# Other PSUM banks for the first two and the last groups of a four-stage transformer pipeline, with the order of both ends written anew

## The reference

```
x = x + cross_attention(ctx, ln(x), mask)        # 8 heads of 16, 77 keys, k and v are the halves of ctx
x = x + s2*(relu2(s1*relu2(s0*[z,-z]@K0)@K1)@K2) # z = ln(x); K0, K1, K2 are +1/-1 matrices, widths 512, 512, 128
x = x + depool(rmsnorm(ln(x))@W_in.T + b_in, rmsnorm(ctx)[..., :128], patch_lens)   # a decaying scan, picked by rank
x = x + top2_of_8_experts(ln(x))                 # softmax gate, 8 experts of 128x128, weighed sum of the best two
```

## Time and profile before

| | |
|---|---|
| median of 3 runs | 553.19 us (551.71 to 553.41) |
| the profiled execution's own time | 553.28 us |
| its span in the trace | 551.5 us |
| TensorE busy | 504.6 us, 92% of the span |
| VectorE busy | 429.6 us, 78% |
| GpSimd busy | 364.2 us, 66% |
| ScalarE busy | 355.7 us, 64% |
| mean granted TensorE clock | 0.982 of full speed |
| DMA | 31 GB/s on average, 16.98 MB |

### The profile page before, as it was taken

The page is one execution under the profiler, slowest core; times in us unless marked ns, Lnnn a source line. Parts: engine busy times, 40 slices in busy tenths (PEclk is TensorE's granted clock), DMA queues, the critical chain, the costliest instruction groups (busy, mean ns, idle before and its releaser), DMA issues.

```text
span 551.5 us, 15070 instructions
## 1 busy us (share of the span) xinstructions
PE 504.6 (92%) x5532; PEld 329.5 (60%) x5532; DVE 429.6 (78%) x1404; ACT 355.7 (64%) x761; POOL 364.2 (66%) x633
## 2 busy tenths in 40 slices
PE   2785898999999999999999999999999999889774
PEld 1565565766666576656676666657665657445531
DVE  7555659888897979797987979797879776865586
ACT  3889567877676867676777768686566565523310
POOL 7874035586868778686868686877758494744554
PEclk9999899999999999999999999999999999999888
DMA  7331001010110101010101001000000000000000
GB/s 167 95 76 43 1 20 50 2 49 21 29 42 20 49 4 49 21 49 22 50 20 49 23 26 44 21 26 3 26 2 8 20 1 22 1 20 1 21 19 19
DMA packets 28503, 16.98 MB, mean 31 GB/s; under 512 B 3687, under 2 KB 28429, under 8 KB 28430
## 3 DMA queue, kind: packets, MB, share of 16 engines
q1 hardware_dynamic: 26670, 15.57, 10.3%
q10 hardware_dynamic: 1760, 0.46, 0.4%
HBM read 11.74 MB, written 4.24 MB: 29 GB/s over the span
## 4 chain that ended last, share of the span: by engine, by line
PE 81%; DVE 7%; ACT 4%; issue 2%; POOL 0%; DVEq 0%; ACTq 0%; POOLq 0%
PE ps L1991 20%; PE ps L1939 20%; PE ps L1884 6%; PE ps L1950 5%; PE ps L1827 5%; PE ps L1901 5%; PE ps L1932 4%; PE ps L1969 3%; PE ps L1970 3%; PE ps L1909 2%; PE ps L1859 2%; DVE weighed L977 2%; PE ps L1982 2%; ACT xn L1480 2%; PE ps L1888 1%
## 5 line engine op out<-in xcount | busy, mean ns | idle before, releaser
L608 POOL TENSOR_TENSOR sum<-weighed 128x512 f32<-128x512 f32 x60 | 76.2, 1270 | 100.3 <-DVE weighed L977 100.3
L1991 PE MATMUL ps<-w_moeT,y4T 128*128 128x512 f32 x256 | 127.3, 624 | 1.5 <-DVE xd L923 0.8
L1939 PE MATMUL ps<-h,w 128*128 128x512 f16 x512 | 118.3, 380 | 2.2 <-DVE att L879 1.2
L977 DVE TENSOR_TENSOR weighed<-ps,wgt 128x1024 f32<-128x1024 f32 x64 | 77.8, 1219 | 42.2 <-PE ps L1991 41.3
L1569 ACT ACTIVATE h<-ps 128x512 f16<-128x512 f32 x128 | 73.7, 591 | 54.2 <-PE ps L1939 33.9
L900 DVE SCALAR_TENSOR_TENSOR h<-ps,h 128x512 f16<-128x512 f32 x128 | 84.7, 681 | 20.1 <-ACT h L1569 20.1
L1939 PEld LDWEIGHTS ps<-h,w 128*128 128x128 f16 x512 | 47.9, 98 | 57.3 <-issue 4.1
L1535 ACT ACTIVATE prT<-ps,maskT 77x1024 f32<-77x1024 f32 x64 | 67.4, 1102 | 16.6 <-PE ps L1888 16.6
L1991 PEld LDWEIGHTS ps<-w_moeT,y4T 128*128 128x128 f32 x256 | 46.7, 195 | 44.7 <-issue 36.9
L560 POOL TENSOR_TENSOR rs<-ve,neg_half 128x4 f32<-128x4 f32 x64 | 65.9, 1030 | 8.7
L848 DVE TENSOR_REDUCE mx<-ps 128x8 f32<-128x616 f32 x64 | 47.7, 786 | 6.3 <-PE ps L1859 6.1
(11 more groups left out here) (169 smaller groups left out, 981.8 us busy)
## 6 DMA issues: line engine op xcount, KB each, us to landing
cx<-in_ctx SPq DMA_DIRECT2D x16, 308.0 KB
xa<-in_x SPq DMA_DIRECT2D x16, 256.0 KB, 3.0
out_x<-xo SPq DMA_DIRECT2D x16, 256.0 KB, 2.3
plugs<-plug_d SPq DMA_DIRECT2D x16, 77.0 KB
nat<-in_L_ffn_W SPq DMA_DIRECT2D x1, 512.0 KB
k_u<-in_L_ffn_k ACTq DMA_DIRECT2D x1, 256.0 KB, 4.8
k_u<-in_L_ffn_k ACTq DMA_DIRECT2D x1, 128.0 KB, 2.5
k_u<-in_L_ffn_k ACTq DMA_DIRECT2D x1, 64.0 KB, 5.6
```

Of the source, the lines that this page charges most:

```text
L608: nc.gpsimd.tensor_tensor(sum4[:], both[:, 0:4 * D], both[:, 4 * D:8 * D], ALU.add).then_inc(c_sum4.sem, 1)
L977: nc.vector.tensor_tensor(weighed[:, j % 2, :].rearrange("p (e d) -> p e d", e=E), pm(g, j).rearrange("p b (e d) -> p (b e) d", d=D), wgt[ ...
L1939: last = pe.matmul(pb(g, k), w2[:, i, c * 128:(c + 1) * 128], h1[:, g.p, part, i, :], start=(i == 0 and part == 0), stop=(i == FC - 1 and ...
L1991: last = pe.matmul(pm(g, j)[:, half, :], y4T[:, g.p, j * S:(j + 1) * S], w_moeT[:, half * 512:(half + 1) * 512], start=True, stop=True)
```

## The change

Banks: g[0]'s attention moves from banks 0 to 3 to banks 4 to 7, and g[1]'s from 4 to 7 to 0 to 3. The turns of the last group move from bank 2 to 0 and its small products from 3 to 1; those of the group before it from 6 and 7 to 4 and 5. The experts of g[13] take two pairs of banks in turn, as g[14]'s did, and the last two pairs of g[15] change places. The lists of all engines are written anew at both ends, and in the middle a few calls change places with their neighbours. What each call does is not changed.

```
         def pa(g):
-            return ps[:, 4:8] if g.n == 1 else ps[:, 0:4]
+            return ps[:, 4:8] if g.n == 0 else ps[:, 0:4]
         def pb(g, k):
             return ps[:, (0 if g.n == NG - 1 else 4) + k % 2, :]
         def pt(g):
-            return ps[:, 2 if g.n == NG - 1 else 6, :]
+            return ps[:, {NG - 1: 0, NG - 2: 4}.get(g.n, 6), :]
         def pp(g):
-            return ps[:, 3 if g.n == NG - 1 else 7, :]
+            return ps[:, {NG - 1: 1, NG - 2: 5}.get(g.n, 7), :]
         def pm(g, j):
             b = 6
             if g.n == NG - 1:
-                b = (2, 6, 0, 4)[j]
-            elif g.n == NG - 2:
+                b = (2, 6, 4, 0)[j]
+            elif g.n >= NG - 3:
                 b = (6, 2)[j % 2]
             return ps[:, b:b + 2]
...
-            make_values()
-            make_ones()
-            a_values_in(g[0])
             rstd(ln_a, g[0])
             a_patch_scale(g[0])
+            rstd(ln_a, g[1])
+            make_values()
             a_patch_normalise(g[0])
-            rstd(ln_a, g[1])
+            a_values_in(g[0])
             make_signs()
             a_patch_scale(g[1])
             make_constants()
-            a_values_in(g[1])
-            a_patch_scale(g[2])
-            make_weights_to_turn()
+            make_ones()
...
+            b_low(g[14], 0)
+            b_residual(g[13])
             e_weigh(g[12], 0)
-            b_residual(g[13])
             c_stats(g[13])
-            b_low(g[14], 0)
+            b_low(g[14], 1)
+            b_low(g[14], 2)
             e_weigh(g[12], 1)
+            b_low(g[14], 3)
+            b_low(g[14], 4)
+            e_weigh(g[12], 2)
             a_weigh(g[15])
             a_residual(g[15])
-            b_low(g[14], 1)
-            b_low(g[14], 2)
-            e_weigh(g[12], 2)
-            b_low(g[14], 3)
-            b_low(g[14], 4)
             b_stats(g[15])
-            c_residual(g[13])
-            a_picks(g[15])
-            d_stats(g[13])
             b_low(g[14], 5)
             b_low(g[14], 6)
-            e_weigh(g[12], 3)
+            c_residual(g[13])
+            a_picks(g[14])
+            d_stats(g[13])
             b_low(g[14], 7)
             b_low(g[14], 8)
+            e_weigh(g[12], 3)
+            b_residual(g[14])
+            c_stats(g[14])
+            b_low(g[15], 0)
             d_gates(g[13])
-            d_top(g[13])
-            b_low(g[15], 0)
-            e_weigh(g[13], 0)
-            b_residual(g[14])
             b_low(g[15], 1)
             b_low(g[15], 2)
-            c_stats(g[14])
+            d_top(g[13])
             b_low(g[15], 3)
             b_low(g[15], 4)
+            e_weigh(g[13], 0)
             e_weigh(g[13], 1)
+            c_residual(g[14])
             b_low(g[15], 5)
             b_low(g[15], 6)
+            d_stats(g[14])
+            a_picks(g[15])
             b_low(g[15], 7)
...
-            turn_weights((a_max[1], g[1]))
+            a_turn_maxima(g[1], (a_max[1], g[1]))
+            a_turn_keys(g[2])
+            a_turn_rows(g[2])
             a_values(g[0])
-            a_turn_rows(g[2], (a_prT[1], g[0]))
-            a_turn_maxima(g[1], (s_weights, g[0]))
-            a_turn_keys(g[2])
+            a_weights(g[1], 0, (a_kT, g[2]), (a_qT, g[2]))
             a_turn_out(g[0])
-            a_weights(g[1], 0)
-            a_scores(g[2], 0, (a_att, g[0]))
             a_weights(g[1], 1, (a_prT[0], g[1]))
-            a_scores(g[2], 1, (a_max[0], g[2]))
-            b_turns(g[0], (a_prT[1], g[1]))
-            a_turn_rows(g[3], (a_max[1], g[2]))
-            a_turn_maxima(g[2])
-            a_turn_keys(g[3])
+            turn_weights((a_att, g[0]), (a_prT[1], g[0]))
+            a_scores(g[2], 0, (a_prT[1], g[1]))
+            b_turns(g[0], (s_weights, g[0]))
+            a_values(g[1], (a_max[0], g[2]))
             b_layer(g[0], 1)
+            a_turn_rows(g[3])
             b_layer(g[0], 2)
...
-            e_experts(g[13], 0, (c_gd, g[13]))
+            d_turns(g[13], (c_weighed, g[12], 4))
+            d_gate_scores(g[13])
             b_layer(g[15], 1)
             b_layer(g[15], 2)
-            e_experts(g[13], 1, (c_weighed, g[13], 1))
+            e_experts(g[13], 0, (c_gd, g[13]))
             b_layer(g[15], 3)
             b_layer(g[15], 4)
+            c_turns(g[14], (b_lo, g[14], 9))
+            e_experts(g[13], 1, (a_prT[1], g[15]))
+            c_project(g[14], (b_x2, g[14]))
             b_layer(g[15], 5)
             b_layer(g[15], 6)
-            c_turns(g[14], (c_weighed, g[13], 2))
             b_layer(g[15], 7)
-            c_project(g[14])
             b_layer(g[15], 8)
-            e_experts(g[13], 2, (c_x3, g[14]), (c_yT, g[14]))
+            e_experts(g[13], 2, (c_weighed, g[13], 1))
             b_last(g[15])
-            e_experts(g[13], 3, (c_weighed, g[13], 3))
-            d_turns(g[14], (c_weighed, g[13], 4))
-            d_gate_scores(g[14])
-            c_turns(g[15], (a_prT[1], g[15]))
-            e_experts(g[14], 0, (c_gd, g[14]))
-            c_project(g[15])
-            e_experts(g[14], 1, (c_x3, g[15]), (c_yT, g[15]))
+            d_turns(g[14], (c_yT, g[14]))
+            e_experts(g[13], 3, (c_weighed, g[13], 2))
+            d_gate_scores(g[14], (c_x3, g[14]))
+            e_experts(g[14], 0, (c_weighed, g[13], 3))
+            c_turns(g[15], (b_lo, g[15], 9))
+            c_project(g[15], (b_x2, g[15]))
+            e_experts(g[14], 1, (c_weighed, g[13], 4))
             e_experts(g[14], 2, (c_weighed, g[14], 1))
             e_experts(g[14], 3, (c_weighed, g[14], 2))
-            d_turns(g[15], (c_weighed, g[14], 4))
-            d_gate_scores(g[15])
-            e_experts(g[15], 0, (c_gd, g[15]))
+            d_turns(g[15], (c_yT, g[15]))
+            d_gate_scores(g[15], (c_x3, g[15]))
+            e_experts(g[15], 0, (c_weighed, g[14], 4))
             e_experts(g[15], 1, (c_weighed, g[14], 3))
-            e_experts(g[15], 2, (b_lo, g[15], 9), (b_x2, g[15]))
-            e_experts(g[15], 3)
+            e_experts(g[15], 2, (c_gd, g[14]))
+            e_experts(g[15], 3, (c_gd, g[15]))
```

More of the change, by code:

```diff
@@ new lines, in _ @@
+            a_weights(g[3], 0, (a_max[1], g[4]))
+            e_experts(g[0], 0, (c_gd, g[0]))
+            b_last(g[1])
+            b_turns(g[2])
+            a_weights(g[3], 1, (a_prT[0], g[3]))
+            e_experts(g[0], 1, (c_weighed, g[0], 1))
+            b_layer(g[2], 1)
+            b_layer(g[2], 2)
+            a_values(g[3])
+            e_experts(g[0], 2, (c_weighed, g[0], 2))
+            a_turn_out(g[3])
+            b_layer(g[2], 3)
+            a_turn_keys(g[5], (a_prT[1], g[3]))
@@ new lines, in _ @@
+            d_gate_scores(g[1])
+            a_weights(g[4], 0, (a_max[1], g[5]))
+            e_experts(g[1], 0, (c_gd, g[1]))
+            b_last(g[2])
+            b_turns(g[3])
+            a_weights(g[4], 1, (a_prT[0], g[4]))
+            e_experts(g[1], 1, (c_weighed, g[1], 1))
+            a_values(g[4])
+            b_layer(g[3], 1)
+            b_layer(g[3], 2)
+            a_turn_rows(g[6], (a_prT[1], g[4]))
+            e_experts(g[1], 2, (c_weighed, g[1], 2))
+            a_turn_out(g[4])
@@ new lines, in _ @@
+            b_layer(g[3], 8)
+            d_gate_scores(g[2])
+            a_weights(g[5], 0, (a_max[1], g[6]))
+            e_experts(g[2], 0, (c_gd, g[2]))
+            b_last(g[3])
+            b_turns(g[4])
+            a_weights(g[5], 1, (a_prT[0], g[5]))
+            e_experts(g[2], 1, (c_weighed, g[2], 1))
+            b_layer(g[4], 1)
+            b_layer(g[4], 2)
+            a_values(g[5])
+            e_experts(g[2], 2, (c_weighed, g[2], 2))
+            a_turn_out(g[5])
+            a_turn_keys(g[7], (a_prT[1], g[5]))
```

1077 lines of the change are left out of this document (748 added, 329 removed).

## The result

| | before | after |
|---|---|---|
| median | 552.45 us (551.11 to 553.41, 4 runs) | 544.69 us (543.95 to 545.42, 4 runs) |
| the profiled execution, its span | 553.28, 551.5 us | 544.96, 543.1 us |

What follows compares the result with a forecast made beforehand. TensorE was taken to bound the middle, chains of waits between engines the two ends. Head 4.5 + tail 8.5 - middle 0.5 = 12.5 us off the profiled 553.28 gave 540.8 us, with an 8-in-10 range of 535 to 549.

Steps and rivals of the forecast that it cites:

- three signs of being wrong: make_constants delays the first a_weights over 2 us; rows from 50 to 58 show the lower level; middle over 361 us.
- Head: Up to a_weights(g[3], 0): fewer waits between engines, gain 4.5 us, bounds 0 and 7.
- Step 1: Head: up to g0's weights, no gain; tail: b_last(g[15]) ends 4.2 to 5.7 us earlier.
- Middle: From a_weights(g[3], 0) to a_weights(g[15], 1): taken as -0.5 us, bounds -3 and +0.6.
- Work and engines stay: Middle: claimed the work and the engines doing it are unchanged there; term taken as -0.5 us.
- fifth rival: Middle: the fourth low half misses layer 5 in nine groups; 558.8 us at 2 us per group; chance 0.08.
- bound of -3: Middle: the unfavourable bound of its term, a loss of 3 us, where -0.5 was taken.
- Tail: From 457.71 us to the end: four steps together gain 8.5 us, bounds 4 and 11.
- Step 2: Tail, to the end of c_project(g[15]): e_experts(g[14], 0) moves in front of c_turns, gain 1.6 to 3.1 us.
- Step 3: Tail, to d_gates(g[15]): VectorE is the chain, e_out(g[14], 3) moves behind the gates, gain 0.8 us.
- Step 4: Tail, last experts: waits before group 15's first two weighings go, gain 1.3 us.
- likeliest case: Head and tail both get shorter as worked out: 540.8 us, own range 536.5 to 545; chance 0.60.

Runs made afterwards that it cites:

- f4_sel: Changed kernel with GpSimd's make_constants moved ahead of scaling the second group's keys: 544.12 us, ratio 0.9835 to before.
- g1_fill: Changed kernel with one TensorE call moved, b_layer(g[2], 8) back between d_turns(g[1]) and d_gate_scores(g[1]): 543.91 us, ratio 0.9831 to before.
- g2_engines_before: g3_both_idle's lists on all engines except TensorE, which keeps the changed kernel's list throughout: 555.64 us, ratio 1.0053 to before.
- g4_experts_late: Changed kernel with e_experts(g[14], 0) put back between c_turns(g[15]) and c_project(g[15]): 546.37 us, ratio 0.9877 to before.
- f3_after: The changed kernel with no edit, run again: 543.91 us, ratio 0.9849 to before.
- e4_middle: Old kernel's head, tail and banks with only the middle passes in the changed kernel's order: 559.61 us, ratio 1.0118 to before.
- g3_both_idle: Changed head and tail, old middle, with group 7's put-off squares and normalisation placed where ScalarE stood idle: 542.88 us, ratio 0.9816 to before.
- e2_head: Changed kernel's head alone, then the old kernel's order, with the old tail's banks and order: 558.72 us, ratio 1.0103 to before.

## Why the prediction was right in sum, and where it was off

The sum came out inside its range with one of its three terms well off. The tail is as told. The head gained by the way told, but less. The middle cost several times what was set for it, and two of the three signs of being wrong that the prediction names did show.

**Head, 4.5 predicted, 3.94 in the first profile, about 2.9 on the mean.** The mechanism is as told: `oT` of g0 at 39.27 (38.6 forecast, 41.33 before), the second exponential of g1 at 46.50 (by 46.5), `b_turns(g[0])` waits for the last of take_weights, which is `w_gateT`, at 51.44 (50.65), `b_layer(g[0], 5)` at 62.35 (59.7, from 68.52), the fixed point at 95.30 (94.7). Step 1 was off: the first weights begin at 26.45 and not at 25.4, and wait 1.86 us for `sel`, just under the 2 us that I had set as a sign of error. Rows of VectorE and GpSimd in the new trace:

```profile
2.79 0.17 DVE L836 TENSOR_SCALAR row_i<-row_i 128x2 int32<-128x2 int32 x1 [2.79 <-POOL zero_s L501]
...
12.87 1.22 DVE L886 TENSOR_TENSOR eighth<-ends_f,step 77x1024 bf16<-77x1024 f32 x1
...
13.06 1.08 POOL L556 TENSOR_TENSOR ve<-mv,eps 128x4 f32<-128x4 f32 x1
14.10 1.24 POOL L557 TENSOR_TENSOR mm<-mv,minus_one 128x4 f32<-128x4 f32 x1
```

VectorE's first operation fell from 1.85 us to 0.17 without the memset beside it, as told. But two small GpSimd operations of group 1, 0.20 us each for group 0, took 1.08 and 1.24 beside VectorE's long operations, and both rstd end at 16.7 and not at 15.7. f4_sel shows that the wait for `sel` was not the cause by itself; `counts` was right behind it. The rows from 50 to 58 did fall to the lower level (granted clock 0.66 from 50 to 60, the values 3.64 us), which I had named as a sign of being wrong. I had made the head's whole gain hang on it, and that was too hard: the level was as low there before (0.68). Over all profiles with the gate scores of g[0] to compare, before's head gives 98.36, 97.76 and 97.55, after's eleven lie from 93.35 to 96.52 (the two of g1_fill and g2_engines_before at 96.20 and 95.00, f4_sel at 94.16 and g4_experts_late at 94.23 among them) with a mean of 95.0: 2.9 us.

**Middle, -0.5 predicted with bounds of -3 and +0.6, and 3.85 us lost in the first profile, 5.1 on the mean.** This is the term that was mis-sized: the price of re-ordering passes that were already full. My criterion "the middle is over 361 us" was met at 362.32, and TensorE was busy 99.4% of it and not over 99.5. From the gate scores of g[0] to those of g[12] before takes 358.47 us, and the four profiles with after's middle unedited 362.32, 364.04, 364.00 and 364.05 (after, f3_after, f4_sel, g4_experts_late). The sentence "Work and engines stay" was wrong too: the set of work of the whole program stays, but not that between the two cuts. The head gains partly by putting off squares, decays and statistics of later groups, and I had counted those as gone from the head without charging them anywhere. ScalarE does 549 instructions in the stretch and not 534, VectorE 997 and not 985. Yet that is not what the 3.3 us hang on, since e4_middle loses them behind a head that owes nothing; what costs there is the order in which the passes were rewritten. The put-off work is a price of its own, shown where before's order was kept: 1.9 us in g3_both_idle. My fifth rival had the right kind of mechanism and the wrong size: a low half behind `b_stats` misses layer 5 once, for 0.42 us in the third pass, against the 2 us per group in nine groups that it needed. It is the only full pass with both the third and the fourth low half behind `b_stats`. The bound of -3 was an opinion about such misses, and both figures lie outside it. What I should have seen is that a pass which leaves TensorE no idle time has no wait that another order could shorten, and many that it could open.

**Tail, 8.5 predicted, 8.31 in the first profile.** Step 1: 53.95 to 49.31, 4.64 gained (4.2 to 5.7). Step 2: from there to the end of `c_project(g[15])` 12.03 to 10.58 (506.93 to 516.88 + 0.63), gain 1.45 with its last matmuls at the lower level (1.6 to 3.1, the lower figure for just that), so just under its range; g4_experts_late undoes it, and the stretch to the gate scores of g[15] gets 2.2 to 2.7 us longer, so this step is shown. Step 3: from there to `d_gates(g[15])` 10.5 to 9.73, gain 0.8 (0.8). Step 4: the rest 17.26 to 15.86, gain 1.4 (1.3). Steps 1, 3 and 4 were only read from the profile, not tried singly. From the gate scores of g[12] to the end the tail of before takes 94.67, 92.83 and 96.49 us (before, e2_head, e4_middle), that of after 86.37 in its first profile and 84.5 on the mean of the ten profiles that have it without an edit: 10.2 us, above what I had taken and within the bound of 11. The first profile had 1.6 us of lower level in it that none of the other nine had.

**The sum.** With these means 2.9 + 10.2 - 5.1 = 8.0 us. The first pair gave 7.8, the later runs on one chip 9.1 between the medians (552.98 for before, 543.91 for f3_after). The likeliest case, that both ends get shorter, is what happened. The profiled execution ended 4.2 us above the point of 540.8 (544.96): 3.35 of it is the middle, 0.56 the head, 0.19 the tail. On the means the tail's 1.7 us above its term make up for the head's 1.6 below, which is luck; the middle's miss of 4.6 stands.

By the rule of the Trainium skill (TensorE: Matmul & The Clock Gate, Part 4) that transposes do not count as activity as matmuls do, I had the head give nothing. It gave 2.9 us. The rows neither confirm nor refute the rule: the turns at 51.44 and the values behind them ran at the lower level, and those of before at 54.06 had done so too.

## What to carry to other kernels

When a start-up is made shorter by putting work off, write down where each put-off instruction is done instead, and price it there. Where hand-written lists on several engines have reached a pass with no idle time on the bound engine, keep that pass call for call and join new ends to it, and look at the joint for calls whose inputs the new head has not made: the five hybrids with after's head and before's middle lost 2 to 10 us there, in one or two stalls each that the timeline names at once. And before a step is moved to shorten a wait, look for the second input: here it was 0.2 us behind.
